# Fewer directly taken gather blocks, and root sums that reach the accumulator by accumulating transfers

## What is computed

```python
out = x @ root + bias
for r in range(8):
    mask = (edge_type == r)
    sums = segment_sum(x[src] * mask[:, None], dst, 1250)
    cnt = segment_sum(mask, dst, 1250)
    out = out + (sums / maximum(cnt, 1)[:, None]) @ weight[r]
u = out
z = concatenate([u, x]) @ w_gate + b_gate
h = tanh(u) * z + x * (1 - z)
```

## Time and profile before

| | |
|---|---|
| profiled execution | 2401.35 us |
| its span, first to last instruction | 2399.6 us |
| mean granted TensorE clock | 0.952 of full speed |
| TensorE busy | 2142.6 us, 89% |
| VectorE busy | 1444.2 us, 60% |
| ScalarE busy | 878.8 us, 37% |
| GpSimd busy | 928.3 us, 39% |
| gather stage | 1021.4 to 1655.4 us of the span |
| dense stage | 1655.6 to about 1819 us |

### The profile page before, as it was taken

One profiled execution on the slowest core, in us unless ns is written; L12 is line 12 of the kernel. 1 busy time (PEld: TensorE's weight loads), 2 busy tenths in 40 slices (PEclk: granted clock), 3 DMA queues, 4 the chain that ended last, 5 costly groups with the idle time before them and its releaser, 6 DMA issues. The chain is left out here.

```text
span 2399.6 us, 29271 instructions
## 1 busy us (share of the span) xinstructions
PE 2142.6 (89%) x9875; PEld 1672.4 (70%) x9875; DVE 1444.2 (60%) x2458; ACT 878.8 (37%) x1149; POOL 928.3 (39%) x846
## 2 busy tenths in 40 slices
PE   7899999999999999699899998998993999999900
PEld 5676777778777888577676676775882888888800
DVE  7467576710100001079999989887986556566577
ACT  3111111111111111155555666664432465555511
POOL 0000056666666400077777777782001110010056
PEclk9999999999999999899999999998995999999955
DMA  5221243322222222488888988863654576766454
GB/s 176 79 74 61 93 134 116 119 86 79 91 84 82 91 79 88 150 294 305 313 276 289 327 299 307 301 217 110 183 172 178 209 284 225 288 246 240 177 210 132
DMA packets 151669, 435.66 MB, mean 182 GB/s; under 512 B 33364, under 2 KB 33748, under 8 KB 151568
## 3 DMA queue, kind: packets, MB, share of 16 engines
q1 hardware_dynamic: 76928, 226.03, 26.9%
q0 software_dynamic: 70016, 190.54, 23.9%
q10 hardware_dynamic: 4624, 17.83, 1.8%
HBM read 382.19 MB, written 80.39 MB: 193 GB/s over the span
## 5 line engine op out<-in xcount | busy, mean ns | idle before, releaser
L185 PE MATMUL psum<-w_hi,xnT_hi 128*128 128x512 f32 (+1 forms) x1600 | 429.7, 403 | 28.7 <-PEq L378 22.7
L185 PE MATMUL psum<-w_lo,xnT_hi 128*128 128x512 f32 (+1 forms) x1600 | 425.6, 396 | 0.0
L176 DVE TENSOR_TENSOR w_lo<-w_raw,w_hi 128x1024 fp32r<-128x1024 f32 x88 | 107.6, 1223 | 526.8 <-ACT w_hi L170 428.0
L185 PE MATMUL psum<-w_hi,xnT_lo 128*128 128x512 f32 (+1 forms) x1600 | 416.3, 394 | 0.0
L475 ACT ACTIVATE work<-psum 128x512 f32<-128x512 f32 (+1 forms) x150 | 89.8, 599 | 766.7 <-PE psum L185 666.6
L185 PEld LDWEIGHTS psum<-w_hi,xnT_hi 128*128 128x128 f32 (+1 forms) x1600 | 297.3, 189 | 99.3 <-issue 26.1
L739 POOL DMA_INDIRECT sorted_rows<-acc x313 | 316.4, 1011 | 116.4 <-issue 85.4
L185 PEld LDWEIGHTS psum<-w_lo,xnT_hi 128*128 128x128 f32 (+1 forms) x1600 | 299.1, 187 | 76.1
L185 PEld LDWEIGHTS psum<-w_hi,xnT_lo 128*128 128x128 f32 (+1 forms) x1600 | 296.7, 185 | 74.5
L832 POOL DMA_INDIRECT w_hi<-y_rows,sort_row x176 | 245.3, 1394 | 60.5 <-issue 53.0
L832 POOL DMA_INDIRECT w_lo<-y_rows,sort_row x176 | 222.2, 1262 | 93.8 <-issue 55.5
(11 more groups left out here) (250 smaller groups left out, 2900.4 us busy)
## 6 DMA issues: line engine op xcount, KB each, us to landing
e_rawbuf<-in_wchunks SPq DMA_DIRECT2D x136, 512.0 KB, 7.2
w_raw<-in_wchunks SPq DMA_DIRECT2D x88, 512.0 KB
y_rows<-work SPq DMA_DIRECT2D x144, 256.0 KB
o_rows<-o_s ACTq DMA_DIRECT2D x17, 1024.0 KB, 7.7
work<-local_rows SPq DMA_DIRECT2D x26, 384.0 KB
b_bc<-in_b SPq DMA_DIRECT2D x17, 512.0 KB, 5.1
acc<-in_bias SPq DMA_DIRECT2D x10, 512.0 KB, 10.9
sorted_rows<-acc POOLq DMA_INDIRECT x313
```

The lines of the kernel that those rows point to most:

```text
L176: v.tensor_tensor(w_lo[:, s, q * PIECE:(q + 1) * PIECE], w_raw[:, q % 2, :], w_hi[:, s, q * PIECE:(q + 1) * PIECE].bitcast(F32), ALU.subtr ...
L185: i = pe.matmul(to[:rm, :], x_[:, k, m * P:m * P + rm], w_[:, s, k * HALF:(k + 1) * HALF], start=(n == 0), stop=(n == 3 * KD - 1))
```

## The change

Two edits. A block is direct once in sixteen instead of once in eight: block 15 of every 16 (22 of 352 instead of 44), so that passes 0, 2, 4, ... have no direct block. The root units are treated as the gate units are: ScalarE copies them out of PSUM into `unit_s`, the sync queue stores them to a new DRAM tensor `root_rows`, and VectorE's additions of them into `acc` are gone. In the dense stage POOL first issues ten accumulating transfers from `root_rows` into `acc`, one for each tile, each waiting for the one ahead of it, and only then the ten that add the gate bias. `transposed` waits for its tile's transfer.

```diff
         def direct(j):
-            return j % SLOTS == SLOTS - 1
+            return j % (2 * SLOTS) == 2 * SLOTS - 1
...
             def _(sp):
                 for i in range(PASSES):
                     for u in ended_before(i):
-                        if u >= 2 * TILES:
-                            m, h = u % TILES, u // TILES - 2
-                            sp.wait_ge(zx_read, u - 2 * TILES + 1)
-                            sp.dma_start(zx_dram[...], zx_s[:rows(m), u % 2, :]).then_inc(zx_stored[u % 2], 16)
+                        m, h = u % TILES, u // TILES % 2
+                        to = zx_dram if u >= 2 * TILES else root_dram
+                        sp.wait_ge(unit_read, u + 1)
+                        sp.dma_start(to[...], unit_s[:rows(m), u % 2, :]).then_inc(unit_stored[u % 2], 16)
...
                         if b == 1:
                             for u in ended_before(i):
-                                if u >= 2 * TILES:
-                                    act.wait_ge(mm_done, RELATION_CHUNKS * TILES + u + 1)
-                                    act.activation(zx_s[...], bank[4 + u % 4][:rows(m), :], ACT.Copy)
+                                act.wait_ge(mm_done, RELATION_CHUNKS * TILES + u + 1)
+                                if u >= 2:
+                                    act.wait_ge(unit_stored[u % 2], 16 * (u // 2))
+                                act.activation(unit_s[...], bank[4 + u % 4][:rows(m), :], ACT.Copy)
...
-                        splits = GROUP - h
+                        splits = GROUP - direct(GROUP * g + GROUP - 1)
...
-                    for u in ended_before(i):
-                        if u < 2 * TILES:
-                            v.wait_ge(mm_done, RELATION_CHUNKS * TILES + u + 1)
-                            accumulate(ROOT_NO[u], acc[:rows(m), m, q * HALF:(q + 1) * HALF], bank[4 + u % 4][:rows(m), :])
...
-                    if u >= 2 * TILES + 4:
-                        pe.wait_ge(zx_read, u - 4 - 2 * TILES + 1)
-                    elif u >= 4:
-                        pe.wait_ge(acc_done, ROOT_NO[u - 4])
+                    if u >= 4:
+                        pe.wait_ge(unit_read, u - 3)
...
             @block.gpsimd
             def _(pool):
                 for s in range(TILES):
+                    if s >= 1:
+                        pool.wait_ge(root_added, 16 * s)
+                    pool.dma_start(acc[:rows(s), s, :], root_dram[s * P:s * P + rows(s), :], accum_op=ALU.add)\
+                        .then_inc(root_added, 16)
+                for s in range(TILES):
                     a, rm = s % 2, rows(s)
                     pool.wait_ge(zx_in[a], 16 * (s // 2 + 1))
...
                 def transposed(m, b, done):
+                    if done is uT_done:
+                        pe.wait_ge(root_added, 16 * (m + 1))
```

More of the change, by code:

```diff
@@ L63, in program @@
         y_dram = nc.dram_tensor("y_rows", (R * N, D), F32, kind="Internal").ap()
+        root_dram = nc.dram_tensor("root_rows", (N, D), F32, kind="Internal").ap()
         zx_dram = nc.dram_tensor("zx_rows", (N, D), F32, kind="Internal").ap()
@@ L774, in ended_before @@
             return [UNIT_AT[i - 1]] if i - 1 in UNIT_AT else []
[L776 to L782, removed]
-            for u in ended_before(i):
-                if u < 2 * TILES:
-                    total += 1
-                    ROOT_NO[u] = total
-        ACC_NO[GROUPS - 1] = total + 1
         with ExitStack() as stage:
@@ L799, in program @@
             lanes, lanes_i = ssb("lanes", [P, P]), ssb("lanes_i", [P, P], I32)
-            zx_s = ssb("zx_s", [P, 2, HALF])
+            unit_s = ssb("unit_s", [P, 2, HALF])
             got = [ssem(f"g_got{b}") for b in range(SLOTS)]
@@ L804, in program @@
                 ssem("g_hi"), ssem("g_hiused"), ssem("g_hot"), ssem("g_scaled"), ssem("g_lo"), ssem("g_pe"))
-            acc_done, zx_read, lanes_done = ssem("g_acc"), ssem("g_zxread"), ssem("g_lanes")
-            zx_stored = [ssem("g_zxst0"), ssem("g_zxst1")]
+            acc_done, unit_read, lanes_done = ssem("g_acc"), ssem("g_unitread"), ssem("g_lanes")
+            unit_stored = [ssem("g_unitst0"), ssem("g_unitst1")]
             block = stage.enter_context(nc.Block())
@@ L812, in _ @@
                     for u in ended_before(i):
-                        if u >= 2 * TILES:
-                            m, h = u % TILES, u // TILES - 2
-                            sp.wait_ge(zx_read, u - 2 * TILES + 1)
-                            sp.dma_start(zx_dram[m * P:m * P + rows(m), h * HALF:(h + 1) * HALF], zx_s[:rows(m), u % 2, :])\
-                                .then_inc(zx_stored[u % 2], 16)
+                        m, h = u % TILES, u // TILES % 2
+                        to = zx_dram if u >= 2 * TILES else root_dram
+                        sp.wait_ge(unit_read, u + 1)
+                        sp.dma_start(to[m * P:m * P + rows(m), h * HALF:(h + 1) * HALF], unit_s[:rows(m), u % 2, :])\
+                            .then_inc(unit_stored[u % 2], 16)
                     for c, q in pieces_in(i):
@@ L822, in _ @@
                 for i in range(2):
-                    sp.wait_ge(zx_stored[i], 16 * TILES)
+                    sp.wait_ge(unit_stored[i], 16 * (UNITS // 2))
             @block.gpsimd
@@ L843, in _ @@
                             for u in ended_before(i):
-                                if u >= 2 * TILES:
-                                    m, n = u % TILES, u - 2 * TILES
-                                    act.wait_ge(mm_done, RELATION_CHUNKS * TILES + u + 1)
[L848 to L851, removed]
+                                m = u % TILES
+                                act.wait_ge(mm_done, RELATION_CHUNKS * TILES + u + 1)
+                                if u >= 2:
+                                    act.wait_ge(unit_stored[u % 2], 16 * (u // 2))
+                                act.activation(unit_s[:rows(m), u % 2, :], bank[4 + u % 4][:rows(m), :], ACT.Copy)\
+                                    .then_inc(unit_read, 1)
                         if b % 2 == 1 and pieces:
@@ L870, in _ @@
                 link(v.tensor_copy(lanes[:, :], lanes_i[:, :]))
[L872 to L876, removed]
                 def flush(g):
@@ L881, in flush @@
                     tile = v.value_load(group_tile[0:1, g:g + 1], min_val=0, max_val=TILES - 1)
-                    accumulate(ACC_NO[g], acc[:, bass.ds(tile, 1), :].rearrange("p o n -> p (o n)"),
-                               psum[:, 2 * (g % 2):2 * (g % 2) + 2, :].rearrange("p b n -> p (b n)"))
+                    if g >= 1:
+                        v.wait_ge(acc_done, g)
+                    at = acc[:, bass.ds(tile, 1), :].rearrange("p o n -> p (o n)")
+                    v.tensor_tensor(at, at, psum[:, 2 * (g % 2):2 * (g % 2) + 2, :].rearrange("p b n -> p (b n)"), ALU.add)\
+                        .then_inc(acc_done, 1)
                 for i in range(PASSES):
@@ L912, in _ @@
                             flush(g - 1)
-                    for u in ended_before(i):
-                        if u < 2 * TILES:
-                            m, q = u % TILES, u // TILES
-                            v.wait_ge(mm_done, RELATION_CHUNKS * TILES + u + 1)
-                            accumulate(ROOT_NO[u], acc[:rows(m), m, q * HALF:(q + 1) * HALF], bank[4 + u % 4][:rows(m), :])
                 flush(GROUPS - 1)
@@ L939, in _ @@
                         if g >= 2:
-                            pe.wait_ge(acc_done, ACC_NO[g - 2])
+                            pe.wait_ge(acc_done, g - 1)
                         pe.wait_ge(hot_done, g + 1)
@@ L995, in program @@
             t_stored, lg_rows = ssem("z_tst"), ssem("z_lgrows")
+            root_added = ssem("z_root")
             zx_shifted = [ssem("z_zxs0"), ssem("z_zxs1")]
```

## The result

The changed kernel takes 2444.01 us (median of 4 runs, 2437.58 to 2446.83) against 2405.6 us before: ratio 1.016, 95% interval 1.0135 to 1.0184. The forecast was 2430 with a range of 2414 to 2452, so the direction and the mechanism held, and 24 us were forecast where 38 were lost. The profiled execution took 2445.13 us with a span of 2443.4, 43.8 us more than the one before.

A forecast was written before the change was run, and what follows sets the result against it. TensorE was taken to pace the gather stage, VectorE close behind, and to be full in the dense stage. 2401.35 - 8 (gather) + 32 (dense) = 2425.4 us profiled; +24 on the median gave 2430 us, range 2414 to 2452.

The forecast's parts named there:

- The chain of ten transfers: Dense stage entry: ten serial root transfers make VectorE wait at tile 0's L1178, +31.0 us; dense stage +32 us.
- a step is 5.1 us, nine steps are 45.9: POOL's root transfers in the dense stage: 5.0 us to land plus about 0.1 to start the next, nine times.
- rival C: Dense stage: slow accumulation from DRAM rows; at 7.5 us a step it loses 54 us, 2452; chance 0.08.
- The slow clock and TensorE's lead cancel: Dense stage after the pause: product 1 already done (2 us) against 2 to 3 us of slow clock; together +1.
- Root additions "buy nothing": Gather stage: taking 0.8 us off VectorE in each of 20 passes buys nothing where TensorE paces.
- The -1.6 us of the two passes with pieces: Gather passes 9 and 20, where VectorE is full: moving the root additions off it gains 1.6 us.
- Fewer direct blocks: Gather stage: split instead of direct blocks gain 0.55 us a pair, -9.9 us over 18 pairs.
- The ceiling: Gather stage: each converted block saves TensorE 0.85 us, at most 20 x 0.85 = 17.0 us.
- TensorE waits about 2 x 0.15 us: Gather stage: two of four borders in a pair lie between groups of four split blocks, costing 0.30 us.
- The four put at +1.0 each: Gather passes 10, 32, 20 and 42, taken as VectorE's: +1.0 us each for the added half, +4.0 in all.
- the -8 us of the gather stage: Gather stage total: -9.9, +4.0 and -1.6 give -7.5, taken as -8 us; ends -17 and +3.
- Rival D: Gather passes without a direct block become VectorE's or POOL's; at +0.5 each, gather stage +13, total 2451; chance 0.05.

The follow-up runs named there:

- The edit alone: Only the second edit, against the kernel before: root sums by ten transfers, a direct block once in eight as before; 2445.66 us, ratio 1.0189.
- the reordering: The changed kernel with gate-bias transfer s issued behind root transfer s+2 instead of behind all ten, one in flight; 2409.0 us, ratio 1.0031 against the kernel before.
- the chain with the one row: The changed kernel with the ten chained transfers reading the one gate-bias row, repeated, instead of root_rows (root sums left out); one run, 2438.16 us.
- the run with the first edit alone: Only the first edit, against the kernel before: a direct block once in sixteen, root units still added by VectorE; 2407.24 us, ratio 1.003.
- the half flush: The changed kernel with the flush adding only the first 512 of 1024 columns of each group's sums; one run, 2423.57 us.

## Why the prediction was right, and where its sizes were off

**The chain of ten transfers: right in place and kind, too short.** The gate-bias transfer stood behind all ten, VectorE waited at tile 0's L1163, TensorE behind product 1, and all behind shifted as it was. The edit alone (ratio 1.0189) and the reordering (30 us back) show it. The term "a step is 5.1 us, nine steps are 45.9" measured 58.8. Of the 12.9 us, 6.4 are the ordinary step (5.8 where 5.1 was taken: 0.5 for real rows, the other 0.2 in landing and wake-up, which the chain with the one row had too), and 6.5 the two long steps while the stage loads its weights and rows. I had these loads in view and priced them at nothing in the sum. The mean step, 58.8 / 9 = 6.5 us, lies between the forecast's 5.1 and rival C's 7.5, which had named both the rows and the loads: part of C came true. The bias's own landing, taken as 5 to 6, was 9.1 us (1712.20 to 1721.30); the tenth root transfer and tile 1's bias were in flight beside it, where before the two bias transfers were issued 3.4 us apart and none took over 6.1. From entry, 31 us were forecast and 47.1 measured.

**The slow clock and TensorE's lead cancel: right.** The granted clock was 0.54 in the pause and 0.82 in the 11 us behind it. Sixteen transposes took 3.67 us (1.91 before, at full clock) and the first eight products 2.44 (2.01), 2.2 us together, and tile 1 still came 12.47 us after tile 0.

**Root additions "buy nothing": right for the kernel before, wrong beside the first edit.** Alone the second edit leaves passes at 13.88 us. The -1.6 us of the two passes with pieces did not come: its gather stage is 633.8 us against 634.0. But with the first edit VectorE paces, and there the root edit is worth 0.70 us a pair, as the run with the first edit alone shows: 28.30 against 27.60. I priced each edit against the old bound.

**Fewer direct blocks: gain 0.17 us a pair, not 0.55.** The ceiling was right (0.85 forecast, 0.89 by the half flush). The step that failed is "TensorE waits about 2 x 0.15 us". I read the border chain as a delay added at two borders. In fact a group of four halves is longer on VectorE than on TensorE, so VectorE falls behind over three such groups in a row, and TensorE waits at three borders and at the second block of the group behind each. The 18 ordinary pairs gave 3.7 us instead of 9.9. The four put at +1.0 each came to +0.4 in all: three of these pairs got shorter, by up to 1.0 us, and only passes 42 and 43 grew, from 29.96 to 31.53 us; why, no run shows. So the -8 us of the gather stage became -3.4, with two errors that partly cancel. Rival D had named VectorE as the one that paces, with a size of the other sign. Its other half, POOL held by the eighth half, did not come: between 1350 and 1450 us its 58 gathers took 76.5 us of issuing, and 78.1 before, and no run shows that a half (1.28 us for 1024 columns) uses a two-port mode at all.

The two errors, 4.6 us in the gather stage and 47.1 - 32 = 15.1 in the dense one, are the distance between the 24 us forecast and the 43.8 of the profiled pair. Over all runs of the comparison the difference is 38 us.

## What to carry to other kernels

When a serial queue takes on new transfers, ask first what stands behind them in program order: here the one that was needed first stood last, and the order alone was worth 30 of 38 us. Price an edit again under the bound that its neighbour makes. Where the pacing engine has little lead on the next, taking work from it moves the bound to that one, and a buffer more between the two can be worth more than the work.

## What the runs showed of the hardware

An accumulating transfer of 512 KB from POOL's queue cost 1.6 us more a step than the same as a plain copy (5.82 and 4.22 us). With the stage's loads beside it a step grew to 9 us; four in flight raised their own landing to 12.3 us and made ScalarE wait 9.5 us for a weight piece, where it waited 4.5 with one in flight. The forecast's sum had nothing for either of these two.
